# Where one load signals, where the scores are copied, and when two weight chunks are rounded, in a kernel of attention and gated norms

## The reference, cut to what matters

```python
def modulated_linear(x, s, aff_w, aff_b, w, b):
    style = s @ aff_w.T + aff_b                       # one vector per batch
    w_mod = w[None] * style[:, None, :]
    demod = rsqrt(sum(w_mod * w_mod, axis=2) + 1e-8)
    return einsum('bni,boi->bno', x, w_mod * demod[:, :, None]) + b

kx = modulated_linear(x, s, k_...).reshape(B, N, 16, 32)
A  = softmax(einsum('bnhd,bnjd->bnhj', kx, kx) / sqrt(32))   # 16x16 per token
x  = x + modulated_linear(einsum('bnhj,bnjd->bnhd', A, kx).reshape(B, N, F), s, o_...)
# second layer, on the new x
h = ln(ln(x) * pw_g[id1] + pw_b[id1]) * cp_g[id2] + cp_b[id2]
t = ln(x) * tm_g[id2] + tm_b[id2];   s = ln(x) * ms_g[id3] + ms_b[id3]
m, n, r = x + (one small MLP with a norm, per batch and kind)
cat = concatenate(w[0]*h, w[1]*t, w[2]*m, w[3]*n, w[4]*r, w[5]*s)   # w = softmax(aw)
x = x + ln(silu(cat @ int_W1 + int_b1) @ int_W2 + int_b2) * int_g + int_be
```

## Time and profile before

| | |
|---|---|
| median of 3 runs | 902.56 us (902.33 to 906.11) |
| the profiled execution | 906.88 us, span 905.0 us |
| TensorE busy | 855.0 us, 94% |
| VectorE, GpSimd, ScalarE busy | 693.0, 630.5, 482.5 us |
| mean granted clock of TensorE | 0.977 of full speed |
| length of step 6 (no weights change) | 49.69 us |
| length of step 7, step 8 | 51.59 us, 51.16 us |

### The profile page before, as it was taken

How to read it: one execution, slowest core, us unless ns; L and a number is a source line. 1 busy time by engine, 2 the same in 40 slices (tenths; PEclk the granted TensorE clock), 3 DMA queues, 4 the chain that set the end, 5 groups by cost and what they waited for, 6 DMA issues and landing times.

```text
span 905.0 us, 19762 instructions
## 1 busy us (share of the span) xinstructions
PE 855.0 (94%) x7474; PEld 772.7 (85%) x7474; DVE 693.0 (77%) x1099; ACT 482.5 (53%) x851; POOL 630.5 (70%) x766
## 2 busy tenths in 40 slices
PE   5986789999999999999999999999999999999987
PEld 5843678999889899999899898999899898999886
DVE  3659677869798878879798878789798877778632
ACT  3565535464655646465555646465545646554521
POOL 2458695878788676877787776868787776757551
PEclk9896999999999999999999999999999999999999
DMA  8961223324434232324434332334333342332110
GB/s 287 417 232 47 59 69 89 101 72 141 103 113 125 72 108 63 111 64 144 101 119 112 83 102 57 112 73 141 98 110 95 84 112 48 110 79 64 40 44 25
DMA packets 104367, 95.56 MB, mean 106 GB/s; under 512 B 72880, under 2 KB 78160, under 8 KB 102608
## 3 DMA queue, kind: packets, MB, share of 16 engines
q1 hardware_dynamic: 95056, 69.26, 26.4%
q0 software_dynamic: 4608, 16.78, 6.6%
q10 hardware_dynamic: 4608, 8.25, 2.7%
HBM read 69.60 MB, written 8.40 MB: 86 GB/s over the span
## 4 chain that ended last, share of the span: by engine, by line
PE 55%; DVE 17%; POOL 11%; issue 8%; ACT 4%; DMA 3%; ACTq 0%; SPq 0%; POOLq 0%; DVEq 0%
PE tok L392 23%; PE acc L392 22%; PE att L392 5%; PE xp L545 4%; POOL op0l L1638 2%; DVE SE L1281 2%; PE xp L392 2%; DMA kb<-in_kb 1%; DVE xb L1377 1%; ACT L892 1%; DVE q L1244 1%; POOL xb L1609 1%; POOL small L1530 1%; DVE small L1277 1%; DVE stg_e L1231 1%
## 5 line engine op out<-in xcount | busy, mean ns | idle before, releaser
L1638 POOL TENSOR_TENSOR op1l<-ytmp,op1h 128x512 fp32r<-128x512 f32 x64 | 86.0, 1343 | 17.9 <-ACT op1h L880 17.5
L1584 POOL TENSOR_TENSOR xlo<-xraw,xhi 128x512 fp32r<-128x512 f32 x31 | 45.8, 1476 | 54.9 <-ACT xhi L775 54.9
L392 PE MATMUL acc<-op0h,W1xh 128*128 128x256 f32 x256 | 76.5, 299 | 1.6 <-DVE op0l L1323 1.6
L392 PE MATMUL acc<-op1h,W1th 128*128 128x256 f32 x256 | 74.9, 293 | 0.0
L1528 POOL TENSOR_TENSOR small<-small,cst 128x1 f32<-128x1 f32 x64 | 22.7, 355 | 73.3 <-DVE small L1319 60.7
L392 PE MATMUL acc<-op1h,W1hh 128*128 128x256 f32 x256 | 73.7, 288 | 0.0
L392 PE MATMUL acc<-op0h,W1sh 128*128 128x256 f32 x256 | 73.7, 288 | 0.0
L392 PE MATMUL acc<-op0l,W1xh 128*128 128x256 f32 x256 | 73.1, 285 | 0.0
L392 PE MATMUL acc<-op0h,W1xl 128*128 128x256 f32 x256 | 73.1, 285 | 0.0
L392 PE MATMUL acc<-op1h,W1tl 128*128 128x256 f32 x256 | 72.4, 283 | 0.0
L392 PE MATMUL acc<-op0h,W1sl 128*128 128x256 f32 x256 | 72.4, 283 | 0.0
(11 more groups left out here) (263 smaller groups left out, 3208.5 us busy)
## 6 DMA issues: line engine op xcount, KB each, us to landing
xsq<-in_x SPq DMA_DIRECT2D x32, 256.0 KB
xb<-in_x SPq DMA_DIRECT2D x32, 256.0 KB, 2.9
out<-xb SPq DMA_DIRECT2D x32, 256.0 KB, 2.1
BD<-q SPq DMA_DIRECT2D x124, 64.0 KB, 2.1
BD<-v SPq DMA_DIRECT2D x124, 64.0 KB
xraw<-in_xT SPq DMA_DIRECT2D x30, 256.0 KB, 2.9
ring<-in_k_wT ACTq DMA_DIRECT2D x6, 256.0 KB, 3.4
dmb<-dm_rows SPq DMA_DIRECT2D x6, 256.0 KB, 3.8
```

What stands on the lines that cost most here:

```text
L392: return e.matmul(o, a, b, start=start, stop=True, skip_group_check=True)
L1584: e.tensor_tensor(xlo[:, :, :], (xraw1 if g == 1 else xraw)[:, :, :], xhi[:, :, :].bitcast(F32), ALU.subtract).then_inc(s["xlo"], 1)
L1638: e.tensor_tensor(op[slot]["l"][:, :, half(g)], four(ytmp[YT[n, g][0]]), op[slot]["h"][:, :, half(g)].bitcast(F32), ALU.subtract).then_inc ...
```

## The change

There are three edits.

1. The load of beint signals c_rp instead of c_ob. The waits for ob and b2 are on 32 of c_ob, the wait for rows_p and the one in front of the first use of beint on 32 of c_rp.
2. On ScalarE, in the steps 3, 7 and 11 and in step 15, `sum_part(b, "S", "Sc")` stands ahead of `z_make(a)` and `bias_2(pa)`, and in the other steps behind them as before.
3. On ScalarE, in the steps 4, 8 and 12, `mod_hi` of the chunks 2 and 3 stands directly behind `a_hi(a)`, ahead of `prod_hi(pa, "s")` and `u_make(pb)`. In the steps 3, 7 and 11 it stands where it was.

```diff
@@ SyncE
-            e.dma_start(beint[:, :], A["int_be"].partition_broadcast(128)).then_inc(s["c_ob"], 16)
+            e.dma_start(beint[:, :], A["int_be"].partition_broadcast(128)).then_inc(s["c_rp"], 16)
@@ ScalarE, bias_2
                 if g == 0:
-                    e.wait_ge(s["c_ob"], 48)
+                    e.wait_ge(s["c_ob"], 32)
@@ ScalarE, loop over k
                 if mod:
                     a_hi(a)
+                    if mod[1] == 1:
+                        mod_hi(*mod, (2, 3))
                 prod_hi(pa, "s")
                 u_make(pb)
...
                 if front:
                     if not mod:
                         a_hi(a)
-                    if mod:
+                    if mod and mod[1] == 0:
                         mod_hi(*mod, (2, 3))
...
                 if front:
-                    z_make(a)
-                    bias_2(pa)
-                    sum_part(b, "S", "Sc")
+                    if mod and mod[1] == 0 or not more:
+                        sum_part(b, "S", "Sc")
+                        z_make(a)
+                        bias_2(pa)
+                    else:
+                        z_make(a)
+                        bias_2(pa)
+                        sum_part(b, "S", "Sc")
@@ VectorE
-            e.wait_ge(s["c_rp"], 16)
+            e.wait_ge(s["c_rp"], 32)
```

## The result

| | median | range | ratio to before | 95% interval |
|---|---|---|---|---|
| kernel before, 15 runs | 903.68 us | 901.62 to 907.16 | | |
| changed kernel, 15 runs | 899.38 us | 897.25 to 901.81 | 0.9942 | 0.9930 to 0.9954 |
| changed kernel on another chip, 6 runs | 900.48 us | 899.79 to 902.10 | 0.9924 | 0.9907 to 0.9941 |

The change makes the kernel faster: by the ratio 5.2 us (4.2 to 6.3) in the first comparison, 6.9 us (5.4 to 8.4) in the second. (The medians of the first lie 4.3 us apart.) The forecast was 8.8 us and 893.8 us, with 898.0 as the upper end; the measured time lies outside its range. The profiled execution took 897.25 us, the lowest of its 15 runs, with a span of 895.5 us, while that of before, 906.88 us, lies near the top of the range of its runs. Their difference of 9.6 us looks like the forecast and is not the result.

The account below looks back on a forecast made before the run. TensorE, busy 94% of 905.0 us, was taken as the bound, except at the start; only its idle pieces could be won. 3.2 + 3 x 1.4 + 1.4 + 0 = 8.8 us off 902.56 gave 893.8 us, range 890.3 to 898.0.

Parts of the forecast that it names:

- The start: Kernel start: without beint's signal add_ob(0) needn't wait, and the exponential starts at 63.75, not 67.00; 3.2 us (0 to 5.67).
- The score copy: Steps 3, 7, 11 and 15: score copy ahead of z on ScalarE saves 1.4 us each (1.05 to 1.9).
- both branches let u_make(a) start about 1.4 us earlier: Step 7: the scaling by 1/sum ends 1.5 us earlier, the statistics branch starts 0.85 earlier with 0.6 to spare.
- VectorE's lock: VectorE with two SBUF operands and GpSimd exclude each other; the copy gives 5.6 us with it, 7.6 without.
- The prediction's own sign of being wrong: Step 7, forecast at about 50.2 us; staying above 50.7 would show the prediction wrong.
- The high parts: Steps 4, 8, 12: the wait for Wo's low part goes but returns at u; 0 us, bounds -0.5 to +0.2 each.
- The sum and its base: Whole kernel: terms of 8.8 us taken off the runs' median 902.56, not the profiled 906.88; 893.8 us.
- (d): Rival: both (b) and (c) hold; gain 4.2 us, 898.4 us, chance 0.07.
- (c): Rival: the start carries nothing, another load ends that wait or the next; 5.6 us alone, 897.0 us, chance 0.14.
- (b): Rival: gather lands early, scaling meets GpSimd's affine pair, 1.05 us a step; gain 7.4, 895.2 us, chance 0.14.
- (a): Rival: high parts pay in steps 4, 8, 12, keeping 0.5 us each; gain 10.3, 892.3 us, chance 0.14.
- (e): Rival: slower, shifted TensorE idle stretches drop its clock to 1.2 GHz in a step; 30 us gives 908.8, chance 0.03.

Follow-up runs that it names:

- e2: Kernel before with only the score copy put ahead of z in steps 3, 7, 11 and 15; ratio to before 0.9973.
- e5b: Kernel before with the first two edits (beint's load signal and score copy), without the third; ratio to before 0.9945.
- e6b: e5b plus GpSimd waiting in steps 3, 7, 11 and 15 for both low parts of silu; ratio to before 0.9945.
- e4: The kernel before, run once more unchanged; ratio 0.9994.
- e3: Kernel before with only the third edit, chunks 2 and 3 of Wo rounded behind the attention's high part; ratio to before 0.9986.
- e10: Changed kernel plus GpSimd waiting for only the first low part of silu, ahead of both scalings; 898.05 us, ratio to before 0.9897.
- e9: Changed kernel plus GpSimd waiting for both low parts of silu in steps 3, 7, 11 and 15; 899.43 us, ratio to before 0.9915.
- e11: The changed kernel run again unchanged, on another chip; 900.48 us, ratio to before 0.9924.
- e1: Kernel before with only the first edit, beint's load signalling c_rp; ratio to before 0.9973.

## Why the prediction was wrong, and where it was right

**The start, 3.2.** Right as a mechanism, in every row that it named: no wait at add_ob(0), the exponential at 63.27 behind the table load, and two ways of removing the wait with the same effect. By the profiles step 3 begins 3.15 us earlier. The timed runs show 1.5 to 2.4. I can't settle the difference: no step in the profiles gives it back, and they are one execution each, those with the edit on average faster and those without it slower than the medians of their runs.

**The score copy, 4 x 1.4 = 5.6.** This is the step that failed. The sum "both branches let u_make(a) start about 1.4 us earlier" held: u's transposes started 1.46 earlier. The gather landed as forecast (issued at 431.94, waited for until 437.06), the scaling ended 44.82 us into the step, where 44.74 was expected, and the wait for e was gone. What failed is the silent next step, that a u 1.4 earlier is a step 1.4 shorter. The prediction applied VectorE's lock to the subtraction and to the scaling and not to the next VectorE instructions of the same kind behind u, the low parts of silu. GpSimd's scaling of Wo comes forward with root2 and meets the first of them, which took 1.04 before and 1.48 now, and x's low part meets the second. The term of 1.4 for a step 3, 7 or 11 measured 0.99 there, less 0.37 in the step behind it, so 0.6; that of step 15 measured 0.9 in e2 and e5b, and 1.3 in the two profiles of the changed kernel (47.28 against 48.62). 3 x 0.6 + 0.9 = 2.8 in place of 5.6. Of the missing 0.4 in the step itself e6b shows the cause by taking it away (50.00). The 0.37 behind it is of the same kind by its place. TensorE's projection with the new Wo starts 29.2 to 29.3 us into the steps 4, 8 and 12 of e2, e5b and the changed kernel, all with both low parts locked, and 28.6 to 28.7 into those steps of the kernel before; in step 12 of e4, behind the locked pair of its step 11, it starts at 29.2 as well. So the second low part puts half a microsecond on that step (51.61 against 51.12 in step 8), and the race for Wo adds to that or hides a part of it. The prediction's own sign of being wrong, a step 7 above 50.7, was just missed by the first profile (50.61) and met by the second (51.61).

The Trainium skill's page SBUF — State Buffer, section "SBUF: two separate sides", has the lock as a rule for any VectorE instruction with two SBUF operands, against a GpSimd instruction that reads SBUF. By that rule the traces agree at three more places: 1.48 and 1.59 for the two low parts of silu, which take 0.69 and 0.65 alone (e6b), and 3.19 for a pair on Wo that otherwise takes 1.81. The prediction ran the rule over two instructions, and not over all that come forward.

**The high parts, 0.** Right when alone (e3: 51.33 against 51.38), and for the reason given. With the copy it is not quite nothing: with it the pair on Wo takes 1.75 to 1.84 us in all six steps of the two profiles of the changed kernel, in e2 and e5b 1.8 to 3.1, and the steps 4, 8 and 12 average 51.52 against 51.75.

**The sum and its base.** "None of the terms lies in that difference, so I take them off the median" set the forecast 1.1 us too low by itself: the median of three runs, 902.56, lay under that of the 15 to which they belong, 903.68, and of the other chips' runs (904.95 to 907.54). So of the 5.6 us between 893.8 and 899.38 the score copy made 2.8 and the base 1.1; the rest, 1.7, is about what the timed runs of the first edit lack of 3.2 (0.8 to 1.7). What can lie in the difference between a profiled execution and the median is the outcome of races and of half-clock stretches. Windows of the tail in the kernel before (columns as in the earlier trace rows):

```profile
860.00:864.00 4.00, 3.35 (x18) 2.42 (x17) 1.81 (x5) 0.79 (x2) 0.74 (x2) 1.00 0.26 102
864.00:868.00 4.00, 2.68 (x15) 2.71 (x16) 1.83 (x3) 1.20 (x2) 3.70 (x6) 0.74 0.17 66
868.00:872.00 4.00, 4.00 (x32) 3.99 (x32) 0.89 (x2) 0.71 (x2) 2.86 (x3) 0.83 0.00 0
```

The granted clock fell to 0.74 and 0.83, so TensorE had 1.2 and not 2.4 GHz for a part of these windows, after it had stood idle in between (busy 2.68 us of 4). In the changed kernel it stayed at 1.00, and not because TensorE did anything else: in the windows of 4 us that begin 4, 8 and 12 us into step 16 it is busy 3.26 to 3.28, 2.97 to 3.01 and 3.03 to 3.08 us in all fourteen profiles, and the clock fell in the third of them in seven profiles and not in the other seven. From the start of step 16 to the end of the span it is 52.6 us with the dip and 50.9 without. The five profiles of kernels with the third edit have none, of the nine without it seven have it. If seven such stretches fell on fourteen profiles at random, all would miss the five about once in 95 times. If that is more than chance it is a gain of up to 1.7 us that none of my steps named, and e3's timed 1.3 us (0 to 2.6) could be it. The edit touches nothing there, the pattern was seen only after the runs, and none of them tests it, so it stays open.

Of the rivals (d), 898.4 us, lies nearest to the measured time and (c), 5.6 us, to the measured gain, but by luck: both let the start carry nothing, and the start came. (b), 895.2 us, names the lock, but at the scaling by the sum, where it fell out as forecast. (a) did not happen. (e) did not happen in the steps 7 and 8; the stretch of half clock in step 2 stands in the profile of before too (granted clock 0.63 in its first 4 us).

## What to carry to other kernels

When a chain is brought forward, list every instruction on both VectorE and GpSimd that comes forward with it, to the end of the step and into the next, and lay the two lists side by side: a lock that was found at one instruction is met again at each of its kind. A step time read from one execution is one draw of several races; two profiles of the kernel before would have shown steps of 51.1 and 51.8 for the same code, and a forecast to 0.5% needs to know that. A wait that keeps two engines apart can pay if it is short (e10, 2.4 us), and can be given back where it makes the waiting engine late for its next meeting (e6b, no gain over e5b).

## What the runs showed of the hardware

- VectorE and GpSimd don't simply take turns by program: GpSimd can get in between two VectorE instructions that stand back to back. A pair on Wo took 1.8 us, or 2.9 to 3.2 with a GpSimd instruction between them (x_lo in e4 and e6b, prod_lo in e9).
- A locked low part of silu took 1.44 to 1.85 us, where 0.65 to 0.69 is its time alone.
- A wait of TensorE that the profile writes as 0.23 us made the product behind it 0.43 to 0.44 us later, at two places.
- TensorE's clock at the head of step 2. Windows of the changed kernel's first profile, then of its second (e11):

```profile
142.57:146.00 3.43, 3.43 (x12) 2.76 (x11) 2.48 (x4) 2.91 (x7) 1.49 (x2) 0.62 0.43 115
```

```profile
142.67:146.00 3.33, 3.33 (x10) 2.66 (x9) 2.47 (x4) 1.93 (x5) 0.41 (x1) 0.50 0.60 169
146.00:150.00 4.00, 4.00 (x27) 3.27 (x26) 0.56 (x1) 1.25 (x5) 3.92 (x5) 0.78 0.14 43
```

A clock of 0.50 is 1.2 GHz for the whole window. In the 4 us just before, TensorE had been busy 2.34 us in the first and 2.21 in e11, and it was full from here on. An estimate of the loss is the missing share times the window: 0.38 x 3.43 = 1.3 us in the first, where step 2 took 50.90, and 0.50 x 3.33 + 0.22 x 4.00 = 2.5 us in the second, where it took 52.32; in e1 step 2 had no such stretch and no wait and took 49.68. The same program need not have it: e10, which is the same up to there, was busy 2.27 of the 4 us before and kept 1.00. So the steps 2 of the fourteen profiles differ by 2.6 us for the same work. The granted clock over step 2 was 0.95 to 0.97 in six of the nine profiles with the first edit and in one of the four without any edit of the load, which goes with the 0.6 us by which step 2 is longer on average. In the other three (e4, e3, e2) the low clock came sooner, 0.57 to 0.63 in the 4 us ahead of step 2, where its cost counts as a later start of the step. So few can't tell that from chance.
